# A third chunk buffer and half-width tiles in the layernorm pass of a fused attention and LoRA layer

## The reference

```python
xn = _layernorm(x, axis=-1)                        # (x - m) / sqrt(v + 1e-5), over the 4096 features
x = x + _L0_attn_ref(xn, w_qkv, w_o) \
      + _L0_ffn_ref(xn, gate, kernel, bias, lora_A, lora_B, lora_A_shared, lora_B_shared)
# attention: 32 query heads, 8 key/value heads of 128, rotary embedding, causal softmax, output projection
# ffn: xn @ kernel + bias + a gated LoRA (16 adapters of rank 32) + a shared LoRA
```

## Time and profile before

| | us |
|---|---|
| time, median of 2 runs | 5480.87 (5325.56 and 5636.18) |
| the profiled execution, its own time | 5244.66 |
| its span on the slowest core (core 3) | 5243.1 |
| spans of the 8 cores | 5198.4 to 5243.1 |
| TensorE busy in the span | 4035.0 (77%) |
| VectorE busy | 1084.8 (21%) |
| ScalarE busy | 955.9 (18%) |

### The profile page before, as it was taken

The page is one execution under the profiler, slowest core; times in us unless marked ns, Lnnn a source line. Parts: engine busy times, 40 slices in busy tenths (PEclk is TensorE's granted clock), DMA queues, the critical chain, the costliest instruction groups (busy, mean ns, idle before and its releaser), DMA issues.

```text
span 5243.1 us, 43617 instructions; the slowest of 8 cores (5198.4 to 5243.1 us)
## 1 busy us (share of the span) xinstructions
PE 4035.0 (77%) x16144; PEld 1528.7 (29%) x16144; DVE 1084.8 (21%) x1618; ACT 955.9 (18%) x913; POOL 511.8 (10%) x790
## 2 busy tenths in 40 slices
PE   2121239993999499948888888888888999949999
PEld 0000014441444244422222222222222344413343
DVE  2132242220111022301121121211212111002222
ACT  2121200000000000003444444444444200000000
POOL 0000000000000000002222222222222100000000
PEclk8565669996999799978888888888888999969999
DMA  6646442316331666451011110111101464386664
GB/s 112 109 88 119 87 146 92 107 53 135 94 106 52 124 101 96 72 98 41 31 37 33 35 37 31 37 33 35 37 31 37 84 111 87 66 170 137 134 128 109
DMA packets 429229, 428.08 MB, mean 82 GB/s; under 512 B 61408, under 2 KB 389344, under 8 KB 428640
## 3 DMA queue, kind: packets, MB, share of 16 engines
q0 software_dynamic: 212352, 223.93, 25.3%
q1 hardware_dynamic: 216672, 201.37, 12.5%
HBM read 503.85 MB, written 83.89 MB: 112 GB/s over the span
## 4 chain that ended last, share of the span: by engine, by line
PE 71%; DVE 10%; DMA 9%; another core or an unknown queue 6%; ACT 2%; issue 1%; SPq 0%; DVEq 0%; ACTq 0%; POOL 0%; POOLq 0%
PE kv_p L86 16%; PE a_rw L81 11%; PE a_av L86 8%; PE w_p L86 8%; PE q_p L86 8%; PE f_p L86 6%; DMA lkv_x<-xTkv 5%; PE a_s L86 4%; DVE a_rc L81 4%; PE a_s L81 3%; DMA f_at<-sc_at 3%; DVE lkv_x L81 2%; DVE lkv_t L81 2%; ACT lkv_q L81 1%
## 5 line engine op out<-in xcount | busy, mean ns | idle before, releaser
L81 ACT ACTIVATE a_p<-a_s,p_btab 128x1024 bf16<-128x1024 f32 x768 | 814.0, 1111 | 2621.9 <-PE a_s L81 2621.9
L86 PE MATMUL a_av<-a_p,a_v 128*128 128x512 bf16 x1536 | 599.2, 390 | 0.0
L81 PE MATMUL a_rw<-a_p,p_onesb 128*1 128x512 bf16 x1536 | 580.0, 378 | 0.0
L86 PE MATMUL f_p<-f_k,f_x 128*128 128x512 bf16 x2048 | 468.0, 388 | 122.1 <-DMA f_x<-sc_xkv 90.6
L86 PE MATMUL kv_p<-kv_w,kv_x 128*128 128x512 bf16 x1984 | 440.6, 380 | 81.5 <-DMA kv_w<-wvT 81.5
L86 PE MATMUL q_p<-q_x,q_w 128*128 128x512 bf16 x1984 | 440.2, 380 | 68.6 <-DMA q_x<-sc_xkv 68.6
L86 PE MATMUL kv_p<-kv_x,kv_w 128*128 128x512 bf16 x1984 | 440.6, 380 | 59.5 <-DMA kv_x<-sc_xkv 59.5
L81 PE MATMUL lkv_ps<-lkv_x,p_onesb 128*1 128x512 bf16 x256 | 106.8, 417 | 458.4 <-ACT lkv_q L81 457.8
L86 PE MATMUL w_p<-w_w,p_attn 128*128 128x512 bf16 x1984 | 441.4, 381 | 2.3 <-SPq L182 2.3
L86 PE MATMUL a_s<-a_q,a_k 128*128 128x512 bf16 x768 | 323.1, 421 | 25.2 <-ACT a_p L81 16.1
L81 DVE TENSOR_TENSOR a_p<-a_p,p_cm 128x512 bf16<-128x512 bf16 x256 | 97.5, 422 | 1168.6 <-ACT a_p L81 1168.6
(11 more groups left out here) (91 smaller groups left out, 2079.5 us busy)
## 6 DMA issues: line engine op xcount, KB each, us to landing
kv_x<-sc_xkv SPq DMA_DIRECT2D x16, 4096.0 KB, 15.4
lkv_x<-xTkv POOLq DMA_DIRECT2D x8, 4096.0 KB, 35.8
sc_xkv<-lkv_x SPq DMA_DIRECT2D x128, 256.0 KB, 2.3
q_w<-wqT POOLq DMA_DIRECT2D x16, 2048.0 KB, 16.5
w_w<-woT POOLq DMA_DIRECT2D x8, 4096.0 KB, 28.8
f_k<-kern POOLq DMA_DIRECT2D x8, 4096.0 KB, 35.7
a_k<-sc_k POOLq DMA_DIRECT2D x384, 64.0 KB, 2.1
a_v<-sc_v POOLq DMA_DIRECT2D x192, 128.0 KB, 2.7
```

What stands on the lines that cost most here:

```text
L81: getattr(eng, m)(*aa, **kk).then_inc(s, st)
L86: getattr(eng, m)(*aa, **kk)
```

## The change

There are three tiles for the chunks instead of two, and the index is `tc % 3` in `do_stats`, in `do_xprime` and for the load. The load of chunk `tc + 1` then waits for chunk `tc - 2`. The slabs of the statistics and of the normalising loop are 512 columns wide instead of 1024 and 32 instead of 16; the broadcast of `bcm` and `bcr` goes away, and there is still one store for two slabs, of 256 KB. `sq` and `tb` are half as large. `p_sum` and `p_sq` are double, and the copies out of them move from `do_stats` to the head of `do_xprime`; statistics of chunk `tc` wait for the copies of chunk `tc - 2` (`row_evac`). The rows `mrow` and `vrow` go away, and their operations work in place in `srow` and `rrow`.

```diff
-            xch = [pp(nc.sbuf_tensor(f"l{tag}_x{i}", [128, 32 * CH], BF16)) for i in range(2)]
-            sq = [pp(nc.sbuf_tensor(f"l{tag}_q{i}", [128, 2 * CH], BF16)) for i in range(2)]
-            tb = [pp(nc.sbuf_tensor(f"l{tag}_t{i}", [128, 2 * CH], BF16)) for i in range(2)]
+            xch = [pp(nc.sbuf_tensor(f"l{tag}_x{i}", [128, 32 * CH], BF16)) for i in range(3)]
+            sq = [pp(nc.sbuf_tensor(f"l{tag}_q{i}", [128, CH], BF16)) for i in range(2)]
+            tb = [pp(nc.sbuf_tensor(f"l{tag}_t{i}", [128, CH], BF16)) for i in range(2)]
...
-            p_sum = pp(nc.psum_tensor(f"l{tag}_ps", [1, CH], F32))
-            p_sq = pp(nc.psum_tensor(f"l{tag}_pq", [1, CH], F32))
+            p_sum = [pp(nc.psum_tensor(f"l{tag}_ps{i}", [1, CH], F32)) for i in range(2)]
+            p_sq = [pp(nc.psum_tensor(f"l{tag}_pq{i}", [1, CH], F32)) for i in range(2)]
...
             def do_stats(tc):
                 nonlocal row_done
-                xi = tc % 2
+                xi = tc % 3
                 ri = tc % 2
                 pe.waitd(xload[xi])
-                pe.wait(s_ve, row_done)
-                for sl in range(16):
-                    si = sl % 2
+                if tc >= 2:
+                    pe.wait(s_ve, row_evac[tc - 2])
+                for dc in range(32):
+                    si = dc % 2
                     ac.waitd(xload[xi])
                     ac.wait(s_pe, qdep[si])
                     av = ac.call("activation", sq[si][:],
-                                 xch[xi][:, sl * 2 * CH:(sl + 1) * 2 * CH], AF.Square)
+                                 xch[xi][:, dc * CH:(dc + 1) * CH], AF.Square)
                     pe.wait(s_ac, av)
-                    for k in range(2):
-                        dc = 2 * sl + k
-                        pe.call("matmul", p_sum[0:1, :], sb_onesb[:, 0:1],
-                                xch[xi][:, dc * CH:(dc + 1) * CH],
-                                start=(dc == 0), stop=(dc == 31))
-                        pq = pe.call("matmul", p_sq[0:1, :], sb_onesb[:, 0:1],
-                                     sq[si][:, k * CH:(k + 1) * CH],
-                                     start=(dc == 0), stop=(dc == 31))
+                    pe.call("matmul", p_sum[ri][0:1, :], sb_onesb[:, 0:1],
+                            xch[xi][:, dc * CH:(dc + 1) * CH],
+                            start=(dc == 0), stop=(dc == 31))
+                    pq = pe.call("matmul", p_sq[ri][0:1, :], sb_onesb[:, 0:1],
+                                 sq[si][:],
+                                 start=(dc == 0), stop=(dc == 31))
                     qdep[si] = pq
                 stats_done[tc] = pe.ctr.v
+
+            def do_xprime(tc):
+                nonlocal row_done
+                xi = tc % 3
+                ri = tc % 2
                 ve.wait(s_pe, stats_done[tc])
                 ve.wait(s_ve, ve.ctr.v)
-                ve.call("tensor_copy", srow[ri][0:1, :], p_sum[0:1, :])
-                row_done = ve.call("tensor_copy", qrow[ri][0:1, :], p_sq[0:1, :])
+                ve.call("tensor_copy", srow[0:1, :], p_sum[ri][0:1, :])
+                row_done = ve.call("tensor_copy", qrow[0:1, :], p_sq[ri][0:1, :])
+                row_evac[tc] = row_done
...
-                for sl in range(16):
-                    ti = sl % 2
+                for dc in range(32):
+                    ti = dc % 2
                     ve.wait(s_ve, tdep[ti])
-                    xs = xch[xi][:, sl * 2 * CH:(sl + 1) * 2 * CH]
-                    v1 = ve.call("tensor_add",
-                                 tb[ti][:].rearrange("p (a t) -> p a t", a=2),
-                                 xs.rearrange("p (a t) -> p a t", a=2), bcm_b)
+                    xs = xch[xi][:, dc * CH:(dc + 1) * CH]
+                    v1 = ve.call("tensor_add", tb[ti][:], xs, bcm[:])
                     ve.wait(s_ve, v1)
-                    v2 = ve.call("tensor_mul",
-                                 xs.rearrange("p (a t) -> p a t", a=2),
-                                 tb[ti][:].rearrange("p (a t) -> p a t", a=2), bcr_b)
+                    v2 = ve.call("tensor_mul", xs, tb[ti][:], bcr[:])
                     tdep[ti] = v2
                     last_tt = v2
-                    sy.wait(s_ve, v2)
-                    stores.append(sy.dma(
-                        out=fview(sc_out)[:, 2 * sl:2 * sl + 2, tc * CH:(tc + 1) * CH],
-                        in_=xs.rearrange("p (a t) -> p a t", a=2)))
+                    if dc % 2 == 1:
+                        sy.wait(s_ve, v2)
+                        stores.append(sy.dma(
+                            out=fview(sc_out)[:, dc - 1:dc + 1,
+                                              tc * CH:(tc + 1) * CH],
+                            in_=xch[xi][:, (dc - 1) * CH:(dc + 1) * CH].rearrange(
+                                "p (a t) -> p a t", a=2)))
...
                 if tc + 1 < nch:
-                    ni = (tc + 1) % 2
+                    ni = (tc + 1) % 3
                     gd.wait(s_ve, xfree[ni])
                     gd.waitd(xstore[ni])
                     xload[ni] = gd.dma(
```

More of the change, by code:

```diff
@@ L215, in ln_pass @@
             pp = ps.enter_context
-            xch = [pp(nc.sbuf_tensor(f"l{tag}_x{i}", [128, 32 * CH], BF16)) for i in range(2)]
-            sq = [pp(nc.sbuf_tensor(f"l{tag}_q{i}", [128, 2 * CH], BF16)) for i in range(2)]
-            tb = [pp(nc.sbuf_tensor(f"l{tag}_t{i}", [128, 2 * CH], BF16)) for i in range(2)]
[L219 to L222, removed]
+            xch = [pp(nc.sbuf_tensor(f"l{tag}_x{i}", [128, 32 * CH], BF16)) for i in range(3)]
+            sq = [pp(nc.sbuf_tensor(f"l{tag}_q{i}", [128, CH], BF16)) for i in range(2)]
+            tb = [pp(nc.sbuf_tensor(f"l{tag}_t{i}", [128, CH], BF16)) for i in range(2)]
+            srow = pp(nc.sbuf_tensor(f"l{tag}_s0", [1, CH], F32))
+            qrow = pp(nc.sbuf_tensor(f"l{tag}_ss0", [1, CH], F32))
             rrow = pp(nc.sbuf_tensor(f"l{tag}_r", [1, CH], F32))
@@ L237, in ln_pass @@
             stats_done = {}
+            row_evac = {}
             def do_stats(tc):
                 nonlocal row_done
-                xi = tc % 2
+                xi = tc % 3
                 ri = tc % 2
                 pe.waitd(xload[xi])
-                pe.wait(s_ve, row_done)
-                for sl in range(16):
-                    si = sl % 2
+                if tc >= 2:
+                    pe.wait(s_ve, row_evac[tc - 2])
+                for dc in range(32):
+                    si = dc % 2
                     ac.waitd(xload[xi])
@@ L273, in do_xprime @@
+                row_evac[tc] = row_done
+                ve.wait(s_ve, row_done)
+                m1 = ve.call("tensor_scalar", srow[0:1, :], srow[0:1, :],
+                             1.0 / D, None, ALU.mult)
                 ve.wait(s_ve, m1)
-                v1 = ve.call("tensor_mul", vrow[0:1, :], mrow[0:1, :], mrow[0:1, :])
+                v1 = ve.call("tensor_mul", rrow[0:1, :], srow[0:1, :],
+                             srow[0:1, :])
                 ve.wait(s_ve, v1)
-                v2 = ve.call("scalar_tensor_tensor", vrow[0:1, :], qrow[ri][0:1, :],
-                             1.0 / D, vrow[0:1, :], ALU.mult, ALU.subtract)
+                v2 = ve.call("scalar_tensor_tensor", rrow[0:1, :], qrow[0:1, :],
+                             1.0 / D, rrow[0:1, :], ALU.mult, ALU.subtract)
@@ L284, in do_xprime @@
                 ve.wait(s_ac, a2)
-                ve.call("tensor_scalar", nrow[0:1, :], mrow[0:1, :], -1.0,
+                ve.call("tensor_scalar", nrow[0:1, :], srow[0:1, :], -1.0,
                         None, ALU.mult)
```

16 lines of the change are left out of this document (4 added, 12 removed).

## The result

The changed kernel is faster: the ratio of its time to that of the kernel before is 0.9533, with a 95% interval of 0.9488 to 0.9577 (its median over 12 runs is 5178.41 us, that of before over 10 runs 5289.52). On the scale of the profiled execution of before, 0.0467 x 5244.7 is 245 us. The forecast was 218 us.

The account below looks back on a forecast made before the run. The first phase was taken as bound by its order and buffers. Two chunks in 44.5 + 26 + 4 + 27.8 + 3 = 105 us start the key phase at 489, not 706.7; 5325.6 - 218 gives 5108 us, range 4990 to 5320.

Parts of the forecast that it names:

- The bound: First phase: bound by its order and buffers, not an engine or bandwidth; POOL waited 564.2 us for stores before loads.
- A load: First phase: a chunk's load takes 34 us alone, 34 + 10.5 = 44.5 us under stores, range 34 to 50.
- The rival of loads that stand still while VectorE normalises: First phase: loads 3, 5 and 7 each cost 18 to 20 us more, total 5085 on the profile's scale; chance 0.11.
- Statistics: First phase, 512 wide: a square takes 0.63 us, two every 1.46, a chunk 26 us against 21.5 before.
- the second rival: First phase: statistics at the low clock throughout, 20 to 30 us more, 5057 on the profile's scale; chance 0.18.
- Normalising: First phase, 512 wide: 32 pairs of VectorE operations at 0.87 us, 27.8 us for a chunk against 22.5 before.
- Row arithmetic: First phase: normalising starts 4 us after the next chunk's statistics instead of 8.3, where VectorE was free.
- The schedule: First phase: load 2 lands at 110, loads 3 and 4 go out at 138 and 174, key phase starts at 489.
- the sum for two chunks: First phase, load 3 to load 5: 44.5 + 26 + 4 + 27.8 + 3 = 105 us.
- The term of 3 us: First phase: from the last normalising operation, the last store's landing and the next load's issue take 3 us.
- The rest of the time: Phases behind the first: code and length unchanged; a rival of granted clock lost there had chance 0.02.
- the lower timed run's scale: Whole kernel: the lower timed run before, 5325.6 us, 81 above the profiled execution; less 218 gives about 5108.

Follow-up runs that it names:

- e1: Changed kernel with two chunk tiles instead of three, narrow slabs and moved copies kept; key phase starts at 741.0 us, against 700.4 in the kernel before.
- e6: Changed kernel with each of its 128 stores made twice, the second into an unread scratch tensor; key phase starts at 553.0 us, against 483.0.
- e3: Kernel before, with normalising of chunk tc - 1 listed ahead of the statistics of chunk tc; key phase starts at 461.3 us, against 700.4.
- c1_after: First profiled execution of the changed kernel, nothing edited; key phase starts at 483.0 us, rest 4498.6 us, slowest core's span 5001.7 us.
- t2_after: Changed kernel, nothing edited, timed again; key phase starts at 478.2 us, ratio 0.9515 to the kernel before.
- e4: Changed kernel with row arithmetic and normalising of chunk tc - 1 listed ahead of the statistics of chunk tc; key phase starts at 437.8 us, against 483.0.
- e5: Kernel before with three tiles, 1024-wide slabs and normalising listed ahead of the next statistics; key phase starts at 434.5 us, against 700.4.
- e2: Kernel before with three chunk tiles, 1024-wide slabs kept, room from four unused rows; key phase starts at 472.6 us, against 700.4.
- the timed ones: Repeat runs of e3's kernel and of the unedited changed kernel (t2_after), timed against the kernel before; ratios 0.9466 and 0.9515.

## Why the prediction was right

**The bound.** Right. One link, a load that waits for the stores of the tile that it overwrites, held the loop closed, and e1 shows it by putting it back: 258 us.

**A load.** Alone 34 us, and under stores 44.5 was taken by adding the stores' share. This was a few us too much. Load 3 took 39.8 to 45.3 us (mean 42.9), 43.83 in the chain above, and loads 4 to 7 took 34.9 to 37.7 in the mean. The same loads with no stores beside them took 34.8 (load 3) and 34.0 to 32.8 (4 to 7) in the kernel before. So the stores cost load 3 about 8 us and the later ones 2 to 4, not 10.5. The rival of loads that stand still while VectorE normalises is out as well: it had load 3 landing at 200, and it landed at 181.2 to 188.6. Load 2 was forecast to land at 110, and landed at 114.0 to 130.5. Stores beside its end alone don't explain that, since in e6, with twice as many, it landed at 111.8 to 117.8.

**Statistics.** The loop of 1.46 us for two squares, with 0.63 for a square taken from a 512-wide Ln, is what the timeline shows to the hundredth. The stretch from the first square to Ln took 24.6 us on core 0, 26 in the forecast. The clock: of chunk 3's statistics the first 7 us ran at the low clock (granted 0.52 from 184.4 to 191.5), and the rest at the high one (1.00 to 209.0), with products 0.21 us apart. So the second rival did not come about here. The Trainium skill ("TensorE: Matmul & The Clock Gate", A second HAM failure mode) warns that short idle times between groups of products can make the clock swing; with two products in each 0.73 us this case shows no swing within a chunk's statistics. The low clock came only behind the waits for a load (ScalarE idle for 14 to 38 us, TensorE for 37.57 before chunk 3).

**Normalising.** 27.8 forecast; 27.7 to 28.1 measured for all eight chunks of core 0, and 22.5 to 22.9 in the kernel before.

**Row arithmetic.** 4 us from the end of the statistics to the loop forecast; 209.02 to 213.51 from the Ln on. That Ln's place behind the next chunk's squares still tied normalising to the next load was seen, but used only to cost the start of the loop. It was the largest thing left: e3 shows that this place alone was worth as much as the third tile.

**The schedule.** Load 3 issued at 138 forecast, 138.8 to 145.3 measured. Load 4 was forecast at 174 and went out at 192.9 to 202.1. This step failed, in its term for the stores. Chunk 1's normalising began at 146.5 to 160.0 instead of 143, because it stood behind the statistics of the late load 2. Above all its stores, 2.3 us each when alone, took 13.9 beside load 3, and the last of them landed 10 to 21 us behind the last normalising operation. The forecast had added the stores' work to the load and left the stores themselves as fast as before. The queue of the loads stood empty for 9 to 14 us behind load 3. The forecast had load 4 waiting in it.

The same step is in the sum for two chunks, and there a second error hides it. Measured are the means over the eight cores, from load 3 to load 7:

| two chunks | forecast | measured |
|---|---|---|
| the load, beside stores | 44.5 | 39.9 |
| statistics | 26 | 24.5 |
| from there to the normalising loop | 4 | 4.3 |
| normalising | 27.8 | 27.9 |
| last stores landing, and the issue | 3 | 8.0 |
| sum | 105 | 104.7 |

The term of 3 us came from stores that land in 2.3 us with no load beside them, and was 5 too small; the load was 4.6 too large and the statistics 1.5. That the sum agrees to 1 us is luck, and e6 shows where the luck ends: with twice the stores the load took 46.6 us and the last term 29.7. The end of the phase was forecast at 489, and came at 483.0 (472.2 to 494.5). The saving, 218 forecast, is 217.4 in this phase.

**The rest of the time.** The forecast left the later phases alone. They are 20 to 21 us shorter in both executions of the changed kernel (c1_after and t2_after), and this is what makes 238 us in the mean of the cores out of 217. What the runs show is a regularity. In the kernel before, the two cores of each pair (0 and 1, 2 and 3, 4 and 5, 6 and 7) reach the key phase 2.6 to 5.5 us apart; in the changed kernel 15.6 to 20.2. Over all kernels, with the mean distance first and the rest of the span behind it: 4.0 and 4543.3 (e4), 4.0 and 4528.6 (e5), 4.5 and 4519.6 (before), 6.9 and 4508.2 (e1), 12.6 and 4510.2 (e6), 17.3 and 4498.6 (changed), 16.8 and 4499.6 (e2), 18.3 and 4499.7 (e3), 17.6 and 4507.2 and 18.5 and 4499.7 (the timed ones). Within a pair the core that is ahead has the shorter rest, in all forty pairs of these ten executions. In the changed kernel's key and value phases, cores 0 and 1 show it in the waits (who for whom, total, times, longest), core 0 first:

```profile
PE kv_p L86 <- DMA kv_x<-sc_xkv: 62.6, 1, 62.6
PE q_p L86 <- DMA q_x<-sc_xkv: 60.3, 1, 60.3
```

```profile
PE f_p L86 <- DMA f_x<-sc_xkv: 79.4, 1, 79.4
PE kv_p L86 <- DMA kv_x<-sc_xkv: 58.9, 1, 58.9
PE q_p L86 <- DMA q_x<-sc_xkv: 56.6, 1, 56.6
```

On core 0 the wait for `f_x` was 87.0, on both cores of the pair in the kernel before 86.8 and 86.5. There the waits for `kv_x` were 56.6 and 59.4, and those for `q_x` 60.8 and 68.1, so not every single wait became shorter. In sum they did: behind the start of the key phase TensorE waited for transfers 365.9 us in the kernel before and 356.4 in the changed one (mean of the cores), while its busy time stayed the same within 3 us (3873.1 and 3870.3). The sum was 353.0 to 356.4 us in the five executions with distances of 16.8 us and more, and 365.9 to 370.8 in the other five. That accounts for about half of the 21 us. e1 and e6 do not fit: their waits are like those of the kernel before (367.3 and 368.2), and still their rests are 11 and 9 us shorter.

A reading that fits most of this is that each phase opens with loads of several megabytes, and that the two cores of a pair slow each other less when they don't ask at once. No kernel was run that changes the distance and nothing else, so this is argued, not shown. It also means that a shorter first phase need not be all gain: e4 and e5 end it 45 to 49 us earlier than the changed kernel with the cores in step, and their rests are 45 and 30 us longer. Of e4's 45, however, some 24 are not waits but products that ran slower in that one execution. The same window on cores 0 and 4:

```profile
500.00:700.00 200.00, 199.05 (x910) 90.69 (x927) 54.94 (x112) 0.00 (x0) 0.00 (x0) 1.00 0.28 93
```

```profile
500.00:700.00 200.00, 200.00 (x763) 82.88 (x762) 47.15 (x96) 0.00 (x0) 0.00 (x0) 0.81 0.24 79
```

On core 4 the granted clock was 0.81 in this window, with TensorE busy all the time, and core 5 shows the same. Their key and value phases were 49 and 52 us longer than in the changed kernel. Behind the start of the key phase TensorE's busy time was 3894.7 us in the mean of e4's cores, against 3870.3. The other execution of e4 was 9 us shorter in the mean of the cores, with a mean granted clock of 0.898 and 0.897 on these two instead of 0.890. Why the clock was lower isn't shown. Without it e4's rest would be near 4519, an estimate from these two busy times, which is that of the kernel before.

**The timed runs.** The forecast of 5108 put the sum on the lower timed run's scale; the median over 12 runs was 5178, and the executions that the ratio uses took 5001 to 5015. The sum itself, on the scale of the profiled execution, was 5027; the profiled execution of the changed kernel took 5003, and most of the difference is the 21 us of the later phases.

## What to carry to other kernels

When a loop without overlap is opened by one more buffer, ask first which list an engine works through in order: here the row arithmetic stood behind the next chunk's work on two engines, and moving two lines gave as much as a third 4 MB tile. Check a sum term by term even where it agrees, since two errors can cancel. If a buffer is paid for with narrower tiles, price each operation's fixed part (0.15 us of 0.42 on VectorE, 0.40 of each 1.46 us in the squares' loop) and look for room that nothing uses before paying. Once transfers overlap, add loads and stores to see the next limit, and expect the small ones, more than the large one, to become slow. A load that waits for such stores then waits longer too.

## What the runs showed of the hardware that was not expected

Stores of 256 KB that land in 2.3 us alone take 13.9 us beside a load of 4096 KB on the other queue (core 0, median), while the load only grows from 35 to 43 us (mean of the cores). With 16 instead of 5 allowed on their way each is slower (16.9 us against 12.9 on core 5), and their queue moves no more (2.21 MB against 2.40 in the same 36 us).

With loads and stores always on their way a core moved 198 GB/s and a chunk of the phase took 48 us, 3.5 us more than the forecast's 34 + 10.5. With twice the stores a chunk took 14 us longer where both queues work.

The distance between the two cores of a pair at the start of the matmul phases goes with some 20 to 30 us in the rest of the kernel, of which some 10 to 15 are TensorE's waits for transfers; the cause isn't isolated.

In one execution (e4) two cores were granted a clock of 0.81 for 200 us with TensorE busy throughout, where another core had 1.00.
